# One Trainium2 core, two transformer layers in float32: the first attention's score tiles, work order and operand layout redone

## What is computed

```
q = einsum('bse,hde->bhsd', x, Wq) + bq      # k and v alike
scores = einsum('bhsd,bhtd->bhst', q, k) / 8
scores = where(causal, -inf, scores)
att = softmax(scores, axis=-1) / 8
z = einsum('bhst,bhtd->bhsd', att, v)
x = x + z.reshape(b, s, 16 * 64) @ proj
```

## Time and profile before

| what | value |
|---|---|
| runs shown | 1166.29, 1170.23, 1177.64 us; median 1170.23 |
| profiled execution, first to last instruction | 1165.7 us |
| TensorE busy (matmul) | 1066.8 us, 92% |
| VectorE busy | 771.7 us, 66% |
| ScalarE busy | 720.5 us, 62% |
| GpSimd busy | 561.7 us, 48% |
| mean granted TensorE clock | 0.953 |
| chain that ended last | PE 58%, DVE 28%, issue 9% |

### The profile page before, as it was taken

The page is one execution under the profiler, slowest core; times in us unless marked ns, Lnnn a source line. Parts: engine busy times, 40 slices in busy tenths (PEclk is TensorE's granted clock), DMA queues, the critical chain, the costliest instruction groups (busy, mean ns, idle before and its releaser), DMA issues.

```text
span 1165.7 us, 17180 instructions
## 1 busy us (share of the span) xinstructions
PE 1066.8 (92%) x5903; PEld 597.7 (51%) x5903; DVE 771.7 (66%) x1549; ACT 720.5 (62%) x1175; POOL 561.7 (48%) x482
## 2 busy tenths in 40 slices
PE   4699999999999999999957799999999589999998
PEld 3445555555555555555537322223222168788876
DVE  5767877877777777787545322235221379999998
ACT  4345655555565565556422499998999476666663
POOL 3356666766667676766720000000000126788786
PEclk9789999999999999999966799999999779999999
DMA  4111111111111111111100000000000002212110
GB/s 115 35 26 37 44 31 38 44 35 33 39 44 26 44 44 26 37 44 37 47 1 1 3 9 11 13 12 11 10 10 10 10 1 93 68 60 86 58 54 37
DMA packets 35290, 40.30 MB, mean 35 GB/s; under 512 B 19652, under 2 KB 22484, under 8 KB 34188
## 3 DMA queue, kind: packets, MB, share of 16 engines
q1 hardware_dynamic: 35212, 39.30, 13.0%
HBM read 19.23 MB, written 1.11 MB: 17 GB/s over the span
## 4 chain that ended last, share of the span: by engine, by line
PE 58%; DVE 28%; issue 9%; ACT 2%; SPq 1%; POOL 1%; DMA 1%; DVEq 0%; ACTq 0%; POOLq 0%
PE banks L1043 10%; PE banks L438 8%; PE banks L1031 6%; PE banks L383 5%; PE banks L423 5%; DVE qb L1348 5%; PE banks L336 4%; PE banks L424 4%; PE banks L459 3%; PE banks L404 3%; DVE kb L619 2%; DVE banks L639 2%; DVE qa L619 2%; DVE zz L668 2%; DVE qb L648 2%
## 5 line engine op out<-in xcount | busy, mean ns | idle before, releaser
L750 POOL TENSOR_TENSOR pacc<-pacc,prob 128x1024 f32<-128x1024 f32 (+3 forms) x160 | 274.6, 1716 | 64.4 <-ACT prob L550 55.1
L1052 ACT ACTIVATE prob<-banks 128x1024 f32<-128x1024 f32 x256 | 238.7, 1099 | 21.4 <-PE banks L1031 21.4
L550 ACT ACTIVATE prob<-banks 128x512 f32<-128x512 f32 (+3 forms) x384 | 167.7, 488 | 110.9 <-PE banks L424 109.1
L1381 POOL TENSOR_TENSOR ka<-prob,qb 128x512 fp32r<-128x512 f32 x108 | 165.1, 1549 | 59.6 <-ACT qb L1331 33.0
L423 PE MATMUL banks<-qa,ka 128*128 128x512 f32 (+3 forms) x384 | 150.6, 400 | 1.4 <-ACT prob L550 1.4
L438 PE MATMUL banks<-prob,v 128*64 128x512 f32 (+3 forms) x768 | 145.0, 498 | 1.0 <-POOL prob L741 1.0
L1337 ACT ACTIVATE prob<-banks,w 128x512 f32<-128x512 f32 x144 | 94.5, 686 | 71.4 <-PE banks L1299 71.3
L1043 PE MATMUL banks<-prob,v 128*32 128x512 f32 x1024 | 137.0, 608 | 0.8 <-DVE pacc L1060 0.3
L997 POOL TENSOR_TENSOR wqkv<-wqkv 64x512 f32<-64x512 f32 x8 | 8.3, 1033 | 260.5 <-DVE wqkv L993 260.5
L424 PE MATMUL banks<-qb,kb 72*128 72x512 f32 (+3 forms) x384 | 131.6, 350 | 0.0
L1031 PE MATMUL banks<-qa,qb 32*128 32x512 f32 x512 | 108.8, 512 | 6.7 <-DVE qb L1018 5.8
(11 more groups left out here) (222 smaller groups left out, 1664.7 us busy)
## 6 DMA issues: line engine op xcount, KB each, us to landing
qb<-qa SPq DMA_DIRECT2D x64, 128.0 KB, 2.3
ka<-ka SPq DMA_DIRECT2D x64, 128.0 KB, 2.3
prob<-gate_rows SPq DMA_DIRECT2D x8, 1024.0 KB, 4.6
w<-in_experts SPq DMA_DIRECT2D x9, 514.0 KB, 3.5
wqkv<-in_wqkv SPq DMA_DIRECT2D x16, 193.0 KB, 2.4
x<-in_x SPq DMA_DIRECT2D x4, 256.0 KB, 3.8
zz<-pacc SPq DMA_DIRECT2D x64, 16.0 KB
wpr<-pacc SPq DMA_DIRECT2D x64, 16.0 KB
```

The costliest lines, as they stand in the source:

```text
L550: act.activation(pr[:, j % NRING, h, 0:wd], banks[:, h, 0:wd], ACT.Exp, scale=SCALE0).then_inc(s_exp, 1)
L750: pool.tensor_tensor(pacc[:, sbk, :, o:BLK], pacc[:, sbk, :, o:BLK], pr[:, j % NRING, :, 0:wd], ALU.add).then_inc(s_padd, 1)
L1052: act.activation(prob[:, n % NP1, :], banks[:, 2 * (n % 3):2 * (n % 3) + 2, :].rearrange("p b c -> p (b c)"), ACT.Exp, scale=2 * SCALE1).t ...
L1381: pool.tensor_tensor(act2[1][:, tb % 2, i, :], hid[:, tb % 2, i, :], act2[0][:, tb % 2, i, :], ALU.subtract).then_inc(s_hlP, 1)
```

## The change

- Scores: the stacked 128-row operands, their ones and shift rows and all copies go. A score tile is now four 64-row matmuls per head (high k by high q, low k by high q, high k by low q, a matrix of ones by the shift rows `mrow`), issued in pairs, head 0 on the upper 64 rows and head 1 on the lower.
- Twelve slots become ten: the diagonal tiles of 384 and 128 columns share a slot. Even slots use banks 0 and 1, odd ones banks 2 and 3. One exp covers both heads.
- Order on TensorE: five times a unit two slots and two maximum runs, all 64-row tiles, then pv, v, sums and out, all column halves. The v projection is split into column halves for this. q/k projections and the transposes stand between the two kinds of run, in the first and the last of the five rounds. All ten maximum runs of unit n now lie in unit u.
- Maxima: even runs in banks 6 and 7, odd ones in banks 0 and 1 behind the exp of the even slot.
- The maxima are transposed as 68 columns, and `mrow_act` writes the shift rows by four ScalarE copies per half, with a column of -1 and 0 as scale.
- pv results are copied from PSUM to SBUF (`zr`) by `z_act` on ScalarE; `sums_pe` then reuses bank 4 or 5, and `z_dve` reads `zr`.
- `hi_act` and `lo_dve` are one operation over 128 partitions each, not two over 64.

```diff
+        SLOTS = ((0, ((0, 0, 0, 512),)), (0, ((1, 0, 128, 384), (3, 384, 384, 128))), (0, ((2, 0, 256, 256),)),
+                 (1, ((0, 0, 0, 512),)), (1, ((1, 0, 0, 512),)), (1, ((2, 0, 0, 512),)), (1, ((3, 0, 0, 512),)),
+                 (1, ((4, 0, 0, 512),)), (1, ((5, 0, 128, 384), (7, 384, 384, 128))), (1, ((6, 0, 256, 256),)))
...
 def scores_pe (body)
+            bank = 2 * (j % 2)
+            for t, at, o, wd in pieces:
+                q, k = slice(half * BLK + o, half * BLK + o + wd), slice(t * P, (t + 1) * P)
+                for h in range(2):
+                    pe.matmul(banks[:, bank + h, at:at + wd], kh[HP[h], w, k], qh[HP[h], w, q], start=True, stop=False)
+                for h in range(2):
+                    pe.matmul(banks[:, bank + h, at:at + wd], kl[HP[h], w, k], qh[HP[h], w, q], start=False, stop=False)
+                for h in range(2):
+                    pe.matmul(banks[:, bank + h, at:at + wd], kh[HP[h], w, k], ql[HP[h], w, q], start=False, stop=False)
+                for h in range(2):
+                    mm = pe.matmul(banks[:, bank + h, at:at + wd], onesr[HP[h], :], mrow[HP[h], w, q], start=False, stop=True)
+            mm.then_inc(s_st, 1)
...
 def unit0_pe (body; first marks the first unit, last the last)
+            for i in range(NS // 2):
+                scores_pe(pe, u, w, 2 * i, first, last)
+                max_pe(pe, n, x_, 2 * i)                      # not in the last unit
+                scores_pe(pe, u, w, 2 * i + 1, first, last)
+                max_pe(pe, n, x_, 2 * i + 1)                  # not in the last unit
                 i == 0: qk 2 and 3 of n, turn_pe(u, 1), pv 8 and 9 of u - 1
                 i == 1: sums of u - 1 second half, pv 0 and 1
                 i == 2: pv 2 and 3, v 0 of n
                 i == 3: out of u - 1, sums of u first half, pv 4 and 5, v 1 of n
                 i == 4: turn_pe(n, 0), qk 0 and 1 of n + 1, pv 6 and 7
...
 def unit0_dve (body)
                 max_dve(n, 2 * i); i == 2: z_dve(u - 1, 1); max_dve(n, 2 * i + 1)
                 i == 0: lo 2 and 3 of n
                 i == 1: newton(u - 1, 1)
                 i == 3: xacc(u - 1), newton(u, 0)
                 i == 4: lo 0 and 1 of n + 1, z_dve(u, 0)
...
+        def mrow_act(act, n, w, half, bank):
+            act.wait_ge(s_turn, 2 * n + half + 1)
+            for s in range(NCH):
+                c = half * BLK + s * P
+                ins = act.activation(mrow[0:MCOLS, w, c:c + P], banks[0:MCOLS, bank, 0:P], ACT.Copy, scale=sel[0:MCOLS, s:s + 1])
+            ins.then_inc(s_mr, 1)
...
+        def z_act(act, u, sbk):
+            act.wait_ge(s_pv, NS * u + (3, NS)[sbk])
+            if u > 0:
+                act.wait_ge(s_zz, 2 * (u - 1) + sbk + 1)
+            act.activation(zr[sbk][:, :], banks[:, 4 + sbk, :], ACT.Copy).then_inc(s_zc, 1)
...
                     ins = dve.tensor_tensor(zz[odd * DH:(odd + 1) * DH, h, sbk * half:(sbk + 1) * half],
-                                            banks[hp, 4 + sbk, odd:BLK:2], yneg[hp, odd:BLK:2], ALU.mult)
+                                            zr[sbk][HP[h], odd:BLK:2], yneg[HP[h], odd:BLK:2], ALU.mult)
```

More of the change, by code:

```diff
@@ L385, in max_pe, with turn_pe @@
             mm.then_inc(s_kp, 1)
[L387 to L391, removed]
-            else:
[L393 to L399, removed]
+        def turn_pe(pe, n, half, bank):
+            pe.wait_ge(s_mx, NR * n + (3, NR)[half])
+            if n == 0 and half == 0:
+                pe.wait_ge(s_cbe, 5)
+            elif half == 0:
+                pe.wait_ge(s_exp, NS * n)
+            else:
+                pe.wait_ge(s_exp, NS * n + 2)
+            pe.transpose(banks[0:MCOLS, bank, 0:P], mx[:, half, :], ident).then_inc(s_turn, 1)
@@ L427, in pv_pe @@
         def pv_pe(pe, u, w, j, first):
-            sbk, t, o, wd = slot_of(j)
-            if masked(j) is None:
-                pe.wait_ge(s_exp, 2 * (12 * u + j + 1))
+            half, pieces = SLOTS[j]
+            g = NS * u + j
+            if j in MASKED:
+                pe.wait_ge(s_msk, NM * u + MASKED[j])
             else:
-                pe.wait_ge(s_msk, 8 * u + masked(j) + 1)
+                pe.wait_ge(s_exp, g + 1)
             if j == 0:
                 pe.wait_ge(s_v, 2 * u + 2)
-            elif j == 4 and not first:
-                pe.wait_ge(s_zz, 2 * u)
@@ L437, in pv_pe @@
-            for h in range(2):
-                mm = pe.matmul(banks[h * DH:(h + 1) * DH, 4 + sbk, o:BLK], v[:, w, t, h * DH:(h + 1) * DH], pr[:, j % NRING, h, 0:wd],
-                               start=(t == 0), stop=(t == (sbk + 1) * 4 - 1))
-            mm.then_inc(s_pv, 1)
-        def sums_pe(pe, u, sbk, first):
-            pe.wait_ge(s_padd, 12 * u + (4 if sbk == 0 else 12))
-            if sbk == 1 or not first:
-                pe.wait_ge(s_nw, 2 * u + sbk)
-            else:
-                pe.wait_ge(s_fc, 13)
-            for h in range(2):
-                mm = pe.matmul(banks[h * DH:(h + 1) * DH, 6, :], ones[:, :], pacc[:, sbk, h, :], start=True, stop=True)
+                if first:
+                    pe.wait_ge(s_lo0, 6)
+                else:
+                    pe.wait_ge(s_nw, 2 * u - 1)
+            elif j == 3 and not first:
+                pe.wait_ge(s_nw, 2 * u)
@@ new lines, in pv_pe, with sums_pe @@
+            for t, at, o, wd in pieces:
+                for h in range(2):
+                    mm = pe.matmul(banks[HP[h], 4 + half, o:BLK], v[:, w, t, HP[h]], pr[:, g % NRING, h, at:at + wd],
+                                   start=(t == 0), stop=(t == 4 * half + 2))
+            mm.then_inc(s_pv, 1)
+        def sums_pe(pe, u, sbk):
+            pe.wait_ge(s_padd, 12 * u + (4, 12)[sbk])
+            pe.wait_ge(s_zc, 2 * u + sbk + 1)
+            for h in range(2):
+                mm = pe.matmul(banks[HP[h], 4 + sbk, :], ones[:, :], pacc[:, sbk, h, :], start=True, stop=True)
@@ L621, in lo_dve, with max_dve @@
-            ins.then_inc(s_lo0, 1)
-        def max_dve(dve, n, r, first):
+            dve.scalar_tensor_tensor(out=(ql, kl)[isk][:, w, c], in0=banks[:, qk_bank(n, i), :],
+                                     scalar=wqkv[:, w, 3 * D + isk:3 * D + isk + 1], in1=(qh, kh)[isk][:, w, c],
+                                     op0=ALU.add, op1=ALU.subtract).then_inc(s_lo0, 1)
+        def max_dve(dve, n, r):
             dve.wait_ge(s_kp, NR * n + r + 1)
-            if r == 0 and not first:
-                dve.wait_ge(s_turn, 2 * (n - 1) + 1)
+            if r == 0 and n > 0:
+                dve.wait_ge(s_turn, 2 * n - 1)
@@ L690, in unit0_dve @@
             n, x_ = u + 1, 1 - w
[L691 to L703 removed]
+            for i in range(NS // 2):
+                if not last:
+                    max_dve(dve, n, 2 * i)
+                if i == 2 and not first:
+                    z_dve(dve, u - 1, 1)
+                if not last:
+                    max_dve(dve, n, 2 * i + 1)
+                if i == 0 and not last:
+                    lo_dve(dve, n, x_, 2)
+                    lo_dve(dve, n, x_, 3)
+                elif i == 1:
```

542 lines of the change are left out of this document (255 added, 287 removed).

## The result

The changed kernel takes **1255.0 us** (median of 4 runs, 1252.1 to 1257.9), the kernel before 1169.2 measured beside it (1166.3 to 1177.6): ratio **1.072**, 95% interval 1.068 to 1.076. The profiled execution spans 1250.3 us, 84.6 more than before's 1165.7. The forecast was 1245 us, in a range of 1165 to 1265, with a chance of 0.66 for slower.

The account below looks back on a forecast made before the run. TensorE was taken to bound each 34.25 us unit; 32.4 + 4.4 + 0.8 + 2.4 = 40.0 us, over 14 units with -1 + 0.9 - 3.6 at the ends, gave +77 on the median 1170.2: 1245 us, range 1165 to 1265.

Parts of the forecast that it names:

- without the contention: Unit with fewer shape changes, small added TensorE work and new waits, but no z delay or slow clock: 32.4 us from 34.25.
- z beside GpSimd: VectorE's two-SBUF z multiplies take turns with GpSimd: +4.4 us a unit before slot 6, +0.8 at the first maximum.
- half clock: After the 5.0 us TensorE gap, half speed for 6 us over slots 6 and 7: +2.4 us a unit.
- rival B: Port not given up between four queued z operations, so only the first waits: unit 35.2, 1180 us; chance 0.20.
- rival C: The z multiply doesn't wait for GpSimd, so 22 fewer shape changes decide: unit 32.4, 1140 us; chance 0.20.
- 1.6 us is harmless: Profile row at 567.20: after 1.59 us idle, TensorE showed no half-speed stretch of matmuls.
- Rival A: z and GpSimd take turns but the TensorE clock holds: unit 37.6, 1214 to 1217 us; chance 0.14.
- Shape changes and waits: On TensorE, 12 array-shape changes a unit instead of 34: -4.2 us; waits 2.8 us where 0.65 was.
- the three waits for exp before an odd maximum: TensorE waits for exp of slots 4, 6 and 8 before odd maxima take banks 0 and 1: 0.2, 0.2, 0.8 us.
- rival D: Row pairs on TensorE don't hide weight loads, 0.32 us a pair not 0.23: +4 a unit, 1200 us; chance 0.04.
- The ends: Outside the repeated units: first unit about -1 us, lead-in +0.9, last unit and tail -3.6.
- The v projection's and the transposes' terms: Added TensorE work a unit: v projection in column halves +0.14 us, two wider transposes +0.1.

Follow-up runs that it names:

- experiment 1: Changed kernel with the Newton step's reciprocal left in its PSUM bank, so z multiplies read one SBUF and one PSUM operand: 1142.5 us, ratio 0.978.
- experiment 4: Changed kernel plus 20 unread 512-column matmuls behind round 2's v projection, filling the large TensorE gap before slot 6: 1215.6 us, ratio 1.040.
- run 5: Not a follow-up run: the fifth maximum run of a unit, on VectorE, which slot 6's scores wait for; 1.23 us in experiment 1.
- Experiment 2: Changed kernel with GpSimd's probability adds cut from up to 512 columns per head to 4, z operands both in SBUF: 1131.2 us, ratio 0.970.
- experiment 3: Kernel before the change, its z multiply reading an unrelated SBUF tensor instead of the pv product in PSUM: 1241.4 us, ratio 1.066.
- 9: Changed kernel with each GpSimd add of both heads issued as two adds of one head, same elements: 1203.2 us, ratio 1.028.
- experiment 10: Kernel of experiment 1 with one pv of each round moved between its two score slots, ten more shape changes a unit: 1167.1 us, ratio 0.998.

## Why the prediction came out right, step by step

| term, us a unit | predicted | shown by | measured |
|---|---|---|---|
| without the contention | 32.4 | 1 | 32.8 |
| z beside GpSimd (gap and first maximum) | 4.4 + 0.8 | 4 less 1 | 37.9 - 32.8 = 5.1 |
| half clock | 2.4 | change less 4 | 40.5 - 37.9 = 2.6 |
| unit | 40.0 | change | 40.5 |

The first two rows take experiment 1 as it stands, and that holds a wait of 0.97 us which its own edit brings, shortly before slot 6. VectorE's run 5 and then TensorE, in experiment 1:

```profile
261.96 1.23 DVE L671 TENSOR_REDUCE mxa<-banks 128x2 f32<-128x1024 f32 x1
```

```profile
262.07 1.08 PE L469 MATMUL banks<-prob,v 128*64 128x512 f32 x4 [0.97 <-DVE zz L697]
262.95 1.07 PE L420 MATMUL banks<-wqkv,xT 128*64 128x128 f32 x16
263.95 0.50 PE L443 MATMUL banks<-big 64*128 64x512 f32 x2
```

Without it TensorE would be at slot 6 at 262.98 and would wait about 0.3 us for run 5, which ends at 263.19. By this estimate the change without contention has a unit of 32.1, and the contention costs 5.8: 4.7 in the gap and 1.0 at the first maximum (1.5 for 0.5). Experiment 2 agrees: its z group takes 2.39 for 1.70 and its wait before slot 6 is 1.0, 0.7 more than 0.3.

Read from the rows the whole sum is: work outside waits 30.7 (experiment 1; I had 29.6), all waits of TensorE 7.1 (60.1 + 18.0 + 6.7 over twelve units; I had 2.8 + 4.4 + 0.8 = 8.0), half clock 2.6 (I had 2.4). The mechanism was forecast; that the unit is within 0.5 us owes something to two misses that cancel.

**The z multiply.** Right in place and order; right in the size of the gap. GpSimd's add, cast, split and add stand in the trace in the forecast order, the gap is 5.05 us for 5.0, and run 5 is what slot 6 waits for. Of the 5.0 I had given 0.6 to run 5 even without contention; by the estimate above it is 0.3, and the slow z brings 4.7. Experiments 1 to 3 show the cause from both engines and in both kernels; 9 refutes rival B (only the first z waits), as do the single rows; 1 is what rival C would have been (1142.5; C said 1140, which the same two misses bring so near). The other z group takes 2.71 for 1.73, 1.0 more for the 0.8 forecast.

**The clock.** The size was right, the shape was not. I said one stretch of 6 us and that a gap of 1.6 us brings none. There are two stretches in most units, 3.4 and 6.8 us, and the first follows a gap of 1.50. Some units have one only and last 39.4 in place of 41.0 (396.40 to 435.76, for one, at a granted clock of 0.94 and not 0.88). My row for "1.6 us is harmless" (567.20) stood in a stage without a large gap beside it; by experiment 4 a gap of 1.5 us is followed by half clock in one unit of twelve without the large gap, and in eight of twelve with it. That 2.6 came out near 2.4 is partly luck. Rival A is refuted: with a 5 us gap the clock doesn't hold, and experiment 4, which is A built, gives 1215.6 for A's 1214 to 1217.

**Shape changes and waits.** These are mis-sized, in opposite directions. Experiment 1 waits 2.1 us a unit, not 2.8, and 0.97 of that is its own wait for z, so the new order brings 1.1 to 1.4; of the three waits for exp before an odd maximum one is there, of 0.6. It spends 30.7 outside waits, not 29.6. So the fewer changes gave about 3.1 and not 4.2. Their number was off too: 34 before counts the transposes as shapes of their own, 12 after does not. Counted alike in the traces they are 34 and 14, so 20 fewer, 0.16 each for my 0.19; experiment 10 says 0.08 to 0.13. The 0.20 between 0.43 and 0.23 was one exit from a score pair, and not every change costs that.

**Row pairs.** They do follow one another at 0.23 (301.39, 301.62, 301.85), so weight loads are hidden although each pair reloads the same rows; rival D is refuted. The rule of the Trainium skill that I weighed against it (TensorE: Matmul & The Clock Gate, "The mechanism"), taken as it stands, doesn't hold here. The same section names a second way for a load to go ahead, a background weight buffer, which I left out; no run here shows which of the two it is.

**The ends.** 84.6 less 14 x 6.23 is -2.6, for -3.7 forecast. No experiment took them apart. Rivals A and C count 15 such units where the forecast counts 14, which is 3 us on A and 2 on C.

Not settled: why the first half-clock stretch is missing in four of twelve units of the changed kernel and there in one of twelve when the large gap is filled. The v projection's and the transposes' terms (+0.24) were never measured by themselves.

## What to carry to other kernels

Before moving an operand from PSUM to SBUF on VectorE, see whether the operation will have two SBUF inputs and what GpSimd runs beside it: here that one operand cost 112 us, ten per cent, and it swallowed a change that is otherwise worth 25. Where it can't be avoided, issue nothing behind it that TensorE waits for, and keep GpSimd's instructions short; both gave back more than half of the loss. After such a gap look at the spacing of the matmuls too, since a third of this loss was the clock, and filler matmuls in idle time gave it back here.

## What the runs showed of the hardware that I had not expected

- GpSimd waits as well: its cast takes 0.60 us for 0.39 and the split 0.78 for 0.64 beside z.
- A GpSimd copy with a single input holds the z multiply too (1.20 us beside a copy of 1.04, experiment 3).
- A TensorE gap of 1.50 us was followed by 3.4 us at half clock in the changed kernel, as in eight of twelve units; where the unit's 5 us gap was filled, a gap of 1.54 us was followed by none in eleven units of twelve.
- Useless matmuls of 4.8 us a unit made the kernel 39 us faster.
